# Local attention of one fused layer chain: column halves, 64-row turns into two banks, all copies by ScalarE

## The reference, cut to what matters

```python
def _layer(x, wqkv, qs, ksc, wo, lg, lb, w1, b1, w2, b2):
    h = shift_token(x)
    q, k, v = jnp.split(h @ wqkv, 3, axis=-1)          # 512 columns each
    q = l2norm(q) * qs;  k = l2norm(k) * ksc
    q, k = rotary_xpos(q, k)
    o = local_attention(q, k, v)                       # each window of 64 sees itself and the one before
    x = x + o @ wo
    h = layer_norm(shift_token(x)) * lg + lb
    a, g = jnp.split(h @ w1 + b1, 2, axis=-1)
    return x + (a * gelu(g)) @ w2 + b2
...
x = _layernorm(x + _L0_ffn_ref(x, ...))
```

## Time and profile before

| | |
|---|---|
| median of 3 runs | 2252.64 us (2249.35 to 2254.05) |
| span of the profiled execution | 2256.5 us (the page gives no other time for it) |
| the changed stage, round 0 to the end of round 31 | about 244 to 620 us of the span |
| PE busy over the span | 2015.2 us, 89% |
| DVE, ACT busy over the span | 1461.1 us (65%), 1170.8 us (52%) |
| mean granted PE clock | 0.964 of full speed |

### The profile page before, as it was taken

One profiled execution on the slowest core, in us unless ns is written; L12 is line 12 of the kernel. 1 busy time (PEld: TensorE's weight loads), 2 busy tenths in 40 slices (PEclk: granted clock), 3 DMA queues, 4 the chain that ended last, 5 costly groups with the idle time before them and its releaser, 6 DMA issues.

```text
span 2256.5 us, 44998 instructions
## 1 busy us (share of the span) xinstructions
PE 2015.2 (89%) x17759; PEld 1190.8 (53%) x17759; DVE 1461.1 (65%) x2920; ACT 1170.8 (52%) x1950; POOL 811.4 (36%) x1153
## 2 busy tenths in 40 slices
PE   7887789999878999998999889999799898999888
PEld 3343456666644454544665344444565665666446
DVE  5775677888778777773555776121677676767474
ACT  2565456656623454555332467332576675757432
POOL 4554333433127748342001321000545344453042
PEclk8999899999998999999999899999999999999999
DMA  3430111111234434210201220000465564655161
GB/s 124 140 111 2 25 32 27 30 32 28 64 108 128 131 91 138 75 34 14 91 1 62 84 84 19 33 0 1 156 208 173 176 207 133 207 175 168 50 127 45
DMA packets 183993, 199.15 MB, mean 88 GB/s; under 512 B 55922, under 2 KB 152486, under 8 KB 179302
## 3 DMA queue, kind: packets, MB, share of 16 engines
q1 hardware_dynamic: 183782, 196.27, 29.6%
HBM read 93.53 MB, written 92.08 MB: 82 GB/s over the span
## 4 chain that ended last, share of the span: by engine, by line
PE 35%; DVE 7%; ACT 6%; issue 2%; DMA 2%; POOL 1%; SPq 1%; DVEq 0%; ACTq 0%; POOLq 0%
PE PS L2134 5%; PE PS L357 4%; PE PS L2383 3%; PE PS L2399 3%; PE PS L2371 3%; PE PS L1985 3%; ACT AR L2543 3%; PE PS L1972 2%; PE PS L1975 2%; PE PS L2737 2%; PE PS L617 1%; PE PS L2725 1%; PE PS L2727 1%; PE PS L596 1%; PE PS L2143 1%
## 5 line engine op out<-in xcount | busy, mean ns | idle before, releaser
L1298 ACT ACTIVATE AR<-PS 128x1024 f32<-128x1024 f32 x160 | 162.5, 1023 | 122.5 <-PE PS L1047 121.6
L739 ACT ACTIVATE AR<-PS 128x1024 f32<-128x1024 f32 x160 | 162.6, 1024 | 92.4 <-PE PS L548 44.5
L1151 DVE TENSOR_REDUCE AR<-PS 128x2 f32<-128x768 f32 (+1 forms) x192 | 159.9, 864 | 52.1 <-PE PS L1026 29.9
L2599 POOL TENSOR_TENSOR RA<-AR,RA 128x288 f32<-128x288 f32 x128 | 88.1, 697 | 275.3 <-DVE RA L2475 141.0
L2543 ACT ACTIVATE AR<-PS,AR 128x512 f32<-128x512 f32 x256 | 173.7, 686 | 23.6 <-DVE AR L2464 23.4
L2464 DVE TENSOR_REDUCE AR<-PS 128x2 f32<-128x1024 f32 x128 | 156.7, 1225 | 12.9
L2371 PE MATMUL PS<-AR 64*128 64x200 f32 (+2 forms) x1280 | 145.9, 352 | 3.5 <-ACT AR L2543 3.5
L1856 POOL TENSOR_TENSOR AR<-AR 128x1024 f32<-128x1024 f32 x32 | 75.4, 2356 | 176.8 <-DVE AR L1704 176.8
L2383 PEld LDWEIGHTS PS<-CC,AR 64*128 64x128 f32 x2048 | 77.4, 140 | 98.3 <-issue 76.5
L2383 PE MATMUL PS<-CC,AR 64*128 64x64 f32 x2048 | 92.0, 229 | 38.9 <-DVE AR L2470 11.5
L2371 PEld LDWEIGHTS PS<-AR 64*128 64x128 f32 x1280 | 110.4, 192 | 7.1 <-ACT AR L2543 3.2
(11 more groups left out here) (370 smaller groups left out, 5043.8 us busy)
## 6 DMA issues: line engine op xcount, KB each, us to landing
ZD<-RC SPq DMA_DIRECT2D x32, 1152.0 KB
AR<-ZD SPq DMA_DIRECT2D x32, 640.0 KB
ZP<-AR SPq DMA_DIRECT2D x128, 160.0 KB, 2.8
SP<-AR SPq DMA_DIRECT2D x40, 384.0 KB, 2.6
AR<-SP SPq DMA_DIRECT2D x128, 96.0 KB
RA<-SP SPq DMA_DIRECT2D x32, 384.0 KB
SP<-AR SPq DMA_DIRECT2D x40, 256.0 KB, 2.9
RC<-RC SPq DMA_DIRECT2D x64, 130.0 KB
```

What stands on the lines that cost most here:

```text
L739: e.activation(self.PT[m % 6], C.PS[:, 2 * s:2 * s + 2, :], ACT.Exp).then_inc(S["s_turned"].sem, 1)
L1151: i = e.tensor_reduce(nm[:, :, 4 * up + q:4 * up + q + 1], src[:, :, a:a + wd], AX, ALU.max, negate=True)
L1298: e.activation(self.PT[m % 6], C.PS[:, 2 * s:2 * s + 2, :], ACT.Exp).then_inc(S["s_turned"].sem, 1)
```

## The change

Four things change in `Local`, and nothing elsewhere but a signature (`among` gets the list of free banks too).

- `lin`, `v`, `hg` and `ha` go through `columns`: two matmuls for output rows 0 to 63 and 64 to 127 in place of one for 128.
- A turn of 128 rows becomes two turns of 64 rows, one from partitions 0 to 63 into one bank, one from 64 to 127 into the next bank. `turnq` and `turnk` become one group of 16 such turns at `turnk`, and the two `flip` steps one group of 16, placed where `flip` 0 was (behind `square` 0 in the plan); `flip` 1 is gone, its four turns stand ahead of `v` now.
- `turnq` and the new `hold` only take a bank. `beside` gives the pair the two neighbouring banks (0 and 1, 2 and 3, 4 and 5 of the six) of which the later was handed out longest ago.
- ACT copies everything: one copy of 128 x 1024 for `flip`, and for `turnk` a copy of its own behind `turnq`, in place of DVE's L1723.

```diff
-                i = line[0] if among is None else [x for x in line if x in among(step)][0]
+                i = line[0] if among is None else [x for x in line if x in among(step, line)][0]
...
-            "t": {"lin": 1, "v": 1, "turnq": 1, "turnk": 1, "scores": 1, "flip": 1, "av": 1, "ot": 1, "out": 1, "two": 1, "hg": 1, "ha": 1, "four": 1, "five": 1, "turnx": 1, "fill": 1},
-            "v": {"init": 1, "lin": 1, "sum": 1, "norm": 3, "turnk": 1, "soft": 2, "av": 2, "out": 1, "ln": 5, "two": 1, "ha": 1,
+            "t": {"lin": 1, "v": 1, "turnq": 0, "turnk": 1, "scores": 1, "hold": 0, "flip": 1, "av": 1, "ot": 1, "out": 1, "two": 1, "hg": 1, "ha": 1, "four": 1, "five": 1, "turnx": 1, "fill": 1},
+            "v": {"init": 1, "lin": 1, "sum": 1, "norm": 3, "soft": 2, "av": 2, "out": 1, "ln": 5, "two": 1, "ha": 1,
                   "four": 1, "add": 1, "fin": 5},
-            "s": {"shift": 1, "square": 1, "v": 1, "norm": 1, "turnq": 1, "exp": 1, "flip": 1, "ot": 1, "ln": 1,
+            "s": {"shift": 1, "square": 1, "v": 1, "norm": 1, "turnq": 1, "turnk": 1, "exp": 1, "flip": 1, "ot": 1, "ln": 1,
                   "hg": 1, "five": 1, "fin": 1, "turnx": 1},
...
+        def beside(step, line):
+            few = many.get(step, range(6))
+            if step[0] in ("turnq", "hold"):
+                return [min((a for a in (0, 2, 4) if a + 1 in few), key=lambda a: max(line.index(a), line.index(a + 1)))]
+            return [line[-1] + 1] if step[0] in ("turnk", "flip") else few
+
+        self.ring = Turns(self.plan[self.head:], 6, {"lin": S["s_square"], "v": S["s_v"], "turnq": S["s_turnk"], "turnk": S["s_turnk"],
+                                         "hold": S["s_flip"], "flip": S["s_flip"], "ot": S["s_ot"], "out": S["v_out"],
                                          "fill": S["t_fill"], "two": S["v_two"], "hg": S["s_hg"], "ha": S["v_ha"], "four": S["v_four"], "five": S["s_five"],
-                                         "turnx": S["s_turnx"]}, lambda step: many.get(step, range(6)))
+                                         "turnx": S["s_turnx"]}, beside)
...
-            if 0 <= n - 1 < N:
-                plan.append(("flip", n - 1, 0))
             if p < N:
                 plan.append(("square", p, 0))
+            if 0 <= n - 1 < N:
+                plan.extend([("hold", n - 1), ("flip", n - 1)])
             if n + 2 < N:
                 plan.extend([("v", n + 2), ("even", n + 2)])
             if p < N:
                 plan.append(("square", p, 1))
-            if 0 <= n - 1 < N:
-                plan.append(("flip", n - 1, 1))
...
+    def pair(self, one, other):
+
+        low = 2 + self.ring.slot[one]
+        assert self.ring.slot[other] + 2 == low + 1
+        return self.C.PS[:, low:low + 2, :]
...
-            e.matmul(o, self.HT[:, L % NB, 64 + 128 * q:192 + 128 * q], W["wqkv" + str(L // NB)][:, 512 * x:512 * x + 512],
-                     start=True, stop=True).then_inc(S["t_" + kind].sem, 1)
-        elif kind in ("turnq", "turnk"):
-            a = 0 if kind == "turnq" else 512
+            columns(e, o, self.HT[:, L % NB, 64 + 128 * q:192 + 128 * q], W["wqkv" + str(L // NB)][:, 512 * x:512 * x + 512],
+                    start=True, stop=True).then_inc(S["t_" + kind].sem, 1)
+        elif kind == "turnk":
+            both = self.pair(("turnq", n), step)
             w.wait_ge(S["g_scale"], n)
-            for c in range(4):
-                i = e.transpose(o[:, 128 * c:128 * c + 128], self.KQ[n % 5][:, a + 128 * c:a + 128 * c + 128], C.ident)
-            i.then_inc(S["t_" + kind].sem, 1)
+            for a in range(8):
+                for x in range(2):
+                    h = slice(64 * x, 64 * x + 64)
+                    i = e.transpose(both[:, x, 64 * a:64 * a + 64], self.KQ[n % 5][h, 128 * a:128 * a + 128], C.ident[h, h])
+            i.then_inc(S["t_turnk"].sem, 1)
...
-            w.wait_ge(S["s_turnq"], n)
-            w.wait_ge(S["v_turnk"], n)
+            w.wait_ge(S["s_turnk"], n)
...
-            a = key[1]
+            both = self.pair(("hold", n), step)
             w.wait_ge(S["s_exp"], n)
-            for c in range(4):
-                i = e.transpose(o[:, 128 * c:128 * c + 128], self.P[n % 2][:, 4 * a + c, :], C.ident)
+            for a in range(8):
+                for x in range(2):
+                    h = slice(64 * x, 64 * x + 64)
+                    i = e.transpose(both[:, x, 64 * a:64 * a + 64], self.P[n % 2][h, a, :], C.ident[h, h])
...
-            w.wait_ge(S["s_flip"], n, 1)
+            w.wait_ge(S["s_flip"], n)
...
-            e.matmul(o, W["w1" + str(L // NB)][:, a:a + 128], self.HN, start=True, stop=True).then_inc(S["t_" + kind].sem, 1)
+            columns(e, o, W["w1" + str(L // NB)][:, a:a + 128], self.HN, start=True, stop=True).then_inc(S["t_" + kind].sem, 1)
...
-        elif kind == "turnk":
-            w.wait_ge(S["v_init"])
-            w.wait_ge(S["t_scores"], n - 3)
-            w.wait_ge(S["t_turnk"], n)
-            e.tensor_copy(self.KT[:, :, 64 + 128 * q:192 + 128 * q], o.rearrange("p (a c) -> p a c", a=4)).then_inc(S["v_turnk"].sem, 1)
...
-            w.wait_ge(S["t_turnq"], n)
-            e.activation(self.QT[n % 2].rearrange("p c t -> p (c t)"), o, ACT.Copy).then_inc(S["s_turnq"].sem, 1)
+            w.wait_ge(S["t_turnk"], n)
+            both = self.pair(step, ("turnk", n))[:, :, 0:256].rearrange("p x (a c) -> p a x c", a=4)
+            e.activation(self.QT[n % 2].rearrange("p a (x c) -> p a x c", x=2), both, ACT.Copy).then_inc(S["s_turnq"].sem, 1)
+        elif kind == "turnk":
+            w.wait_ge(S["v_init"])
+            w.wait_ge(S["t_scores"], n - 3)
+            q = n % 4
+            both = self.pair(("turnq", n), step)[:, :, 256:512].rearrange("p x (a c) -> p a x c", a=4)
+            e.activation(self.KT[:, :, 64 + 128 * q:192 + 128 * q].rearrange("p a (x c) -> p a x c", x=2), both, ACT.Copy).then_inc(S["s_turnk"].sem, 1)
...
-            a = key[1]
             w.wait_ge(S["t_av"], n - 2)
-            w.wait_ge(S["t_flip"], *key)
-            e.activation(self.PT[n % 2][:, 4 * a:4 * a + 4, :].rearrange("p c j -> p (c j)"), o, ACT.Copy).then_inc(S["s_flip"].sem, 1)
+            w.wait_ge(S["t_flip"], n)
+            both = self.pair(("hold", n), step).rearrange("p x (c j) -> p c x j", c=8)
+            e.activation(self.PT[n % 2].rearrange("p c (x j) -> p c x j", x=2), both, ACT.Copy).then_inc(S["s_flip"].sem, 1)
```

More of the change, by code:

```diff
@@ L312, in flags @@
                 keys = [s[1:] for s in plan if s[0] == step]
-                if keys:
+                if keys and per:
                     out[engine + "_" + step] = self.flag(engine + "_" + step, keys, per)
@@ L928, in __init__ @@
         self.slots = Turns(self.plan, 3, {"scores": S["v_scores"], "turned": S["s_turned"]},
-                           lambda step: range(2 if step[0] == "scores" and step[1] < 11 else 3))
+                           lambda step, line: range(2 if step[0] == "scores" and step[1] < 11 else 3))
         self.seven = Turns(self.plan, 1, {
@@ L1474, in __init__ @@
         many.update({step: range(5) for step in self.plan[late:last]})
-        self.ring = Turns(self.plan[self.head:], 6, {"lin": S["s_square"], "v": S["s_v"], "turnq": S["s_turnq"], "turnk": S["v_turnk"],
-                                         "flip": S["s_flip"], "ot": S["s_ot"], "out": S["v_out"],
+        def beside(step, line):
[5 more added lines that the diff above has]
+                                         "hold": S["s_flip"], "flip": S["s_flip"], "ot": S["s_ot"], "out": S["v_out"],
                                          "fill": S["t_fill"], "two": S["v_two"], "hg": S["s_hg"], "ha": S["v_ha"], "four": S["v_four"], "five": S["s_five"],
-                                         "turnx": S["s_turnx"]}, lambda step: many.get(step, range(6)))
+                                         "turnx": S["s_turnx"]}, beside)
         self.past = ((S["v_lin"], 31, 1), (S["t_lin"], 31, 1), (S["g_sum"], 31), (S["v_sum"], 31), (S["s_square"], 31, 1),
@@ L1731, in on_vector @@
             w.wait_ge(vs, n, part=1)
-            w.wait_ge(S["t_flip"], n - 2, 1)
+            w.wait_ge(S["t_flip"], n - 2)
             e.tensor_tensor(self.P[n % 2], s, m.unsqueeze(2).broadcast_to((128, 8, 128)), ALU.subtract).then_inc(vs.sem, 1)
@@ L2259, in __init__ @@
                                          "vals": S["v_vals"], "wt": S["s_wt"], "wo": S["v_wo"], "turnx": S["s_turnx"]},
-                          lambda step: range(2 if step in few else 3))
+                          lambda step, line: range(2 if step in few else 3))
         self.past = ((S["s_exp"], 127), (S["v_scores"], 127), self.ring.held[2])
@@ L2677, in __init__ @@
             S["y_rep", r] = C.flag(f"y_fetch{r}", [(b,) for b in range(r, NB, 2)], 32)
-        self.slots = Turns(self.plan, 3, {"hidden": S["v_hidden"]}, lambda step: range(2 if step[1] < 5 else 3))
```

(1 more changed line is left out.)

## The result

The changed kernel takes **2289.0 us** in the median of 4 runs (2286.61 to 2291.96), against 2253.35 us for the kernel before on the same chip (4 runs, 2249.35 to 2257.21). The ratio is 1.0167 with a 95% interval from 1.0149 to 1.0184: slower, by 36 us. I had forecast 2271 us, with a range up to 2284. The side was right, the loss was twice what I had worked out.

What follows compares the result with a forecast made beforehand. The prediction took PE as the bound: a round is PE's list of work plus at most 1.0 us ahead of the mask. Waits 18, other rounds -2 and clock 2 gave +18 us on 2252.6: 2271 us, range 2254 to 2284.

Steps and rivals of the forecast that it cites:

- kind C: Rounds 10, 14, 18, 22, 26: flips wait for `square` of the queries, +0.9 us each.
- kind A: Rounds 8, 12, 16, 20, 24: flips wait for `square` of the queries, `hg` follows `v`, +0.6 us each.
- kind B: Rounds 9, 13, 17, 21, 25: flips don't wait, `hg` waits for `square` of the keys, +0.15 us each.
- kind E: Rounds 2 to 6, without feed-forward: the turns wait for `square` of the keys, +0.5 us each.
- kind D: Rounds 11, 15, 19, 23, layer norm ahead of `lin`: flips and turns both wait for `square`, +1.8 us each.
- Part 4: New waits of PE for `square` through the paired banks: 18.0 us in all, -2 for the other eight rounds.
- Part 5: PE's clock falling with the longer pauses of rounds 11, 15, 19, 23: between 0 and 5 us, taken as 2.
- Parts 2 and 3: On PE, 64-row turns save 22 us; five more changes of tile shape a round cost 16 us.
- Part 1: Products by halves in `lin`, `v`, `hg` and `ha`: no faster, 0 us for 144 products.
- Part 6: DVE's lost copy and ACT's added copies cost nothing; ACT goes from 62% to 66% busy.
- Nothing new is waited for: Rival: banks come free in time, only turn savings and shape changes count, 2247 us, faster; 11%.
- The clock falls often: Rival: 8 more rounds with pauses of 1.3 to 1.6 us fall in clock by 1.5 us, 2283 us; 14%.

Runs made afterwards that it cites:

- r2: The changed kernel with a pair of banks free to start at any bank, not only 0, 2 and 4: 2266.16 us.
- t4: The changed kernel with both squares ahead of the flip copy on ACT, pairs still at banks 0, 2 and 4: 2265.67 us.
- s5: The changed kernel with pairs starting at any bank and both squares ahead of the flip copy on ACT: 2255.32 us.
- s7: The changed kernel with twelve idle matmuls on PE ahead of the flips in rounds 11, 15, 19 and 23: 2283.52 us.
- t3: The kernel before with both squares ahead of the first flip copy on ACT: 2249.30 us.
- r1: The kernel before with only `lin`, `v`, `hg` and `ha` as two column halves: 2255.28 us.
- s8: The changed kernel with the copy of `turnk` back on DVE, behind ACT's copy of the queries: 2288.04 us.
- r4: The changed kernel with `lin`, `v`, `hg` and `ha` as whole products, 64-row turns kept: 2278.05 us.
- r3: The changed kernel with whole products and full 128-row turns, its order, bank pairs and ACT copies kept: 2281.59 us.

## Why the prediction was right on the side and wrong in the size

The spans differ by 2287.8 - 2256.5 = 31.3 us; the other 4 us of the 36 are that the profiled execution of before was further above its median (with 1.9 us around the span, as in the execution after: 2289.74 for 2287.8, it would be 2258.4). By the steps of the prediction, in us (the measured ones are the rounds of the kinds, after less before, in the profiles):

| step | forecast | measured |
|---|---|---|
| kind C, five rounds | 4.5 | 5.6 |
| kind A, five | 3.0 | 4.1 |
| kind B, five | 0.8 | 2.3 |
| kind E, five | 2.5 | 4.1 |
| kind D, four, without the clock (1.75 each, by round 15) | 7.2 | 7.0 |
| the other rounds, and outside of them (forecast: eight rounds alone) | -2 | -1.6 |
| clock (three rounds of kind D, less before's round 11: 7.0; round 2: 2.8) | 2 | 9.8 |
| sum | 18 | 31.3 |

The clock fell in other rounds too, in both kernels, and those falls stand in the row of the other rounds: before in 0, 1 and 7 (11.3 us at the low clock), after in 1, 27 and 28 (11.0 us, and 6.0 in round 2). Over rounds 0 to 30 it was low for 40.8 us and before for 14.7; at 0.36 us for one the difference is 9.4, an estimate near the 9.8 of the table.

- **What bounds the kernel: right.** A round is PE's list plus its waits; all that PE lost is in the span.
- **Part 4, the waits: right in place and nearly in size.** 14 waits of the flips, 1.2 to 1.3 us each and 2.8 in kind D, the turns in D and E and `hg` in B (0.6 us), where I had put them. (That the six banks go round ten times in a round is a slip: some ten steps of a round take a bank each. No term rests on it.) Undoing the pairs (r2) and the order on ACT (t4) takes 16.1 and 17.7 us from the stage, both together (s5) 31.5: they are the whole of the 30.2, with the part of the clock that hangs on them.
- **Part 5, the clock: this step failed.** The mechanism was named, its size was not: 9.8 us for 2, the largest single part of the 13 us that were missing. I had bounded it by 5 us and took 2, reckoning that a fall costs at most 1.7 us of a 3.4 us stretch and that part of that falls on waiting. It was low for 6.8 us twice and for 10.2 once in kind D, 2.4 to 3.5 us a round, and the low stretch of round 19 begins at 488.0, 0.8 us behind the end of PE's wait, and so falls on its list of work and not on the wait. (In round 19 of r2 it begins at 475.5, inside the wait that ends at 476.40; so the reckoning isn't wrong everywhere.) With 9.8 in place of 2 my sum would be 26 and the time 2278, inside my range. s7 shows the cost by itself: the same wait, PE kept busy, 2.5 us less in round 23 (14.86 for 17.34).
- **Parts 2 and 3, the shapes: the second step that failed, mis-sized by some 6 us.** I had 22 us of gain less 16 of loss. A change of shape costs more than the 0.1 that I read from `out` to `av`. In round 14 of r2, where nothing waits, it can be seen bare: `ot` 0.58 (406.83 - 406.25) for 0.43 in the earlier trace rows, sixteen turns 0.64 for 0.52 in the earlier trace rows, `v` 1.01 for 0.87. The two `flip` groups thus cost 0.64 + 0.15 = 0.79 for 0.86 before, a gain of 0.07 and not of 0.35. The pair that shows the account is t3 and s5. Both have the squares first and no wait of the flips for `square`, and s5 has the new shapes, pairs and copies: the seventeen rounds named at r1 take 185.1 us in t3 and 185.0 in s5. Nothing won, nothing lost. The kinds C, A, B and E are over the forecast by 1.1 to 1.6 us each, 5.3 together, which is about the gain of 6 us that I had counted; that the one explains the other is a count, and no run tests it kind by kind. The Trainium skill says in "TensorEngine Tiling (Array Packing)", Key Properties, that a switch of mode drains TensorE. The trace agrees in that a group costs more beside another shape, and the price is paid at both ends of a group (0.15 us in `ot`, 0.12 in the turns).
- **Part 1, the halves: 0 was nearly right for the product, with its changes of shape it costs some.** r1 has a ratio of 1.0013 (0.9998 to 1.0028), and its rounds of kinds E, A, B and C lose 0.12 to 0.32 us each.
- **Part 6, ACT and DVE: right for the copy** (s8: no difference), **and half right for ACT.** It is not full, as I said, but the order in which it works is worth 17.7 us of the stage. I named that in the forecast of B, D and E and did not ask what it was worth to turn it round.
- **The rivals.** "Nothing new is waited for" and "cancel" are excluded by the waits. "The clock falls often" has the nearest number, 2283, but not the right place: I had expected rounds of kinds C, A and E to fall. In the changed kernel these stay at full clock with waits of 1.2 to 1.5 us; of the rounds with a wait of 2.8, three in four fell. Such a short wait isn't safe for all that: in s7, and in round 11 of r2, the clock is low in `lin` right behind a wait of 1.3.

## What to carry to other kernels

Where a group of steps must have neighbouring buffers, look up who holds them last, and let the pair begin anywhere: that one line was worth 16 us of the stage, more than any shape of matmul. On an engine that copies for TensorE, put the copy that TensorE waits for ahead of the long one that nobody wants yet; this gained on the kernel before, too. Price a new wait of TensorE of about 3 us with the clock that may fall behind it (here 2.4 us a round), not with its length alone, and fill it with idle matmuls if it can't be had shorter.

## What the runs showed of the hardware

- The same waits in the same order gave a fall of the clock in rounds 11, 19 and 23, and none in round 15. In r4 and s8, with the same waits, it is round 11 that is spared, and in r3 none is. What makes the difference stays open; it was not tried.
- Sixteen 64-row turns into two banks cost 0.52 us in a row of their like the earlier trace rows, and 0.64 between groups of another shape, to which 0.15 comes in the group ahead: eight full turns cost 0.87. A shape that is faster among its like wins next to nothing in a short group between others.
- How long a low clock lasted doesn't follow from the waits. It was 6.8 us in rounds 19 and 23 of the changed kernel, with a second wait of 1.3 us inside it, and 3.4 us in t4, where that wait is gone. But in round 19 of r2 it was 6.8 us with no wait of PE behind the one of 3.12 (the line below, clock 0.51), and in round 15 of r3, with both waits, 3.4 us.

```profile
475.50:482.30 6.80, 5.89 (x60) 5.27 (x60) 2.94 (x5) 4.23 (x6) 3.83 (x2) 0.51 0.17 39
```
